# Another written-out order of the same steps on every engine of an RWKV-7 layer with a SwiGLU FFN

## What is computed

```
S_t = S_{t-1} * diag(exp(w_t)) + (S_{t-1} a_t) b_t^T + v_t k_t^T
y_t = S_t r_t          # then group norm, bonus term, gate, @ w_output.T
```

## Time and profile before

| | |
|---|---|
| device time, median of 3 runs | 1608.94 us (1607.33 to 1612.72) |
| span of the profiled execution | 1603.4 us |
| PE busy | 1520.5 us, 95% |
| DVE busy | 1243.6 us, 78% |
| ACT busy | 1069.5 us, 67% |
| POOL busy | 354.6 us, 22% |
| chain that ended last | PE 92%, DVE 3%, ACT 2% |

### The profile page before, as it was taken

One profiled execution on the slowest core, in us unless ns is written; L12 is line 12 of the kernel. 1 busy time (PEld: TensorE's weight loads), 2 busy tenths in 40 slices (PEclk: granted clock), 3 DMA queues, 4 the chain that ended last, 5 costly groups with the idle time before them and its releaser, 6 DMA issues.

```text
span 1603.4 us, 48245 instructions
## 1 busy us (share of the span) xinstructions
PE 1520.5 (95%) x20288; PEld 1064.9 (66%) x20288; DVE 1243.6 (78%) x2661; ACT 1069.5 (67%) x1889; POOL 354.6 (22%) x362
## 2 busy tenths in 40 slices
PE   3699999999999999999999999999999999999887
PEld 1366767576676757667676676757667675766765
DVE  2968787787878878887887878778787887888643
ACT  3758586685857758685775858668585775768512
POOL 3121402313040131302213140231304013130201
PEclk9799999999999999999999999999999999999999
DMA  4011110301212021111202111030121202111020
GB/s 149 14 25 29 33 34 16 62 18 32 43 25 47 16 55 25 33 34 24 56 16 39 42 34 34 16 62 19 33 42 25 48 16 55 25 33 34 12 56 28
DMA packets 251430, 57.85 MB, mean 36 GB/s; under 512 B 223696, under 2 KB 250704, under 8 KB 251088
## 3 DMA queue, kind: packets, MB, share of 16 engines
q1 hardware_dynamic: 241936, 41.95, 13.9%
q10 hardware_dynamic: 9280, 12.81, 2.2%
HBM read 36.38 MB, written 18.35 MB: 34 GB/s over the span
## 4 chain that ended last, share of the span: by engine, by line
PE 92%; DVE 3%; ACT 2%; issue 1%; POOL 0%; DMA 0%; SPq 0%; ACTq 0%; DVEq 0%; POOLq 0%
PE bank L534 23%; PE chunk L380 15%; PE bank L544 11%; PE bank L509 8%; PE bank L664 4%; PE chunk L642 3%; PE chunk L614 3%; PE chunk L589 3%; PE chunk L598 2%; PE bank L485 2%; PE bank L380 2%; PE bank L517 2%; PE bank L479 2%; PE chunk L628 2%; DVE VU L981 1%
## 5 line engine op out<-in xcount | busy, mean ns | idle before, releaser
L1325 POOL TENSOR_TENSOR SF<-ST,CT 128x256 f32<-128x256 f32 x128 | 99.7, 779 | 728.8 <-DVE ST L1211 728.8
L534 PE MATMUL bank<-xT,wg 128*128 128x256 f32 x768 | 197.2, 391 | 14.2 <-DVE VU L981 13.5
L534 PE MATMUL bank<-xT,wu 128*128 128x256 f32 x768 | 207.3, 395 | 0.0
L544 PE MATMUL bank<-wd,hT 128*128 128x256 f32 x768 | 176.8, 383 | 1.9 <-DVE hT L1171 1.9
L534 PEld LDWEIGHTS bank<-xT,wg 128*128 128x128 f32 x768 | 136.3, 189 | 57.6 <-DVE VU L981 24.1
L544 PEld LDWEIGHTS bank<-wd,hT 128*128 128x128 f32 x768 | 143.3, 190 | 29.3 <-issue 7.2
L534 PEld LDWEIGHTS bank<-xT,wu 128*128 128x128 f32 x768 | 135.1, 188 | 34.8 <-issue 14.5
L380 PE MATMUL chunk<-KS,W 128*128 128x512 f32 x320 | 149.6, 598 | 0.3 <-ACT gT L719 0.3
L509 PE MATMUL bank<-qpad,KS 128*64 128x32 f32 x4096 | 141.2, 226 | 4.0 <-DVE KE L1143 4.0
L887 ACT ACTIVATE Y<-chunk 32x256 f32<-32x256 f32 x256 | 96.3, 376 | 70.9 <-PE chunk L598 67.0
L509 PEld LDWEIGHTS bank<-qpad,KS 128*64 128x64 f32 x4096 | 130.7, 141 | 14.1 <-issue 9.0
(11 more groups left out here) (156 smaller groups left out, 3231.3 us busy)
## 6 DMA issues: line engine op xcount, KB each, us to landing
smalls<-in_x SPq DMA_DIRECT2D x32, 256.0 KB, 3.1
Y<-in_x SPq DMA_DIRECT2D x32, 256.0 KB, 3.0
out<-fsil ACTq DMA_DIRECT2D x32, 256.0 KB, 2.6
scrA<-AM SPq DMA_DIRECT2D x64, 64.0 KB, 1.9
hat<-scrB SPq DMA_DIRECT2D x32, 128.0 KB, 3.1
hat<-scrF SPq DMA_DIRECT2D x32, 128.0 KB, 3.1
KE<-scrA SPq DMA_DIRECT2D x64, 32.0 KB, 2.2
scrT<-KE SPq DMA_DIRECT2D x16, 128.0 KB, 1.7
```

Of the source, the lines that this page charges most:

```text
L534: q = pe.matmul(o[:, TT_ * n2:TT_ * n2 + TT_], w[:, h, 128 * (n + n2):128 * (n + n2) + 128], x_now[:, h], start=(h == 0), stop=(h == NH - 1))
L544: q = pe.matmul(o[:, 256 * m:256 * m + 256], hT[:, n, 128 * m:128 * m + 128], wd[:, n, :], start=(n == 0), stop=(n == NF - 1))
L1325: pool.tensor_tensor(SF[:, :, :, :], ST[:, :, :, :], fade[:, c].unsqueeze(3).to_broadcast([128, B, NH, N]), ALU.mult).then_inc(*faded.up)
```

## The change

```diff
-ORDER = {"pe": ("NNNFNKOOFNNORVNNNNKKOVKRBNKBNRNNVBBNBBNBNBNBBVNNBBEBVBBNBBVBNBBNBBXBXBBNXBBNBNBBXBBXBXBBNBBLBNBBXXBB"
-            "LXXXXLL"),
-         "act": ("NFKFFFFFRFVNKKNVOKKKBEBOKRKRDXXBXBVNBVNBBVVNBBBXBVVBBXBBBBNBBXXBLBBLXLBXBBNBBLXX"),
-         "dve": ("ONBOOBBBBBDBBBBBBBNBBDBBDDOOKKDXEFKKNDEDEXDKEEBXBXXXNBXBXXXBEXXBEXXBXNBXLBXXXBXXBLXBXNXXXBXXXBXLXLBX"
-             "XXBBXXLLLLLLLL"),
-         "pool": ("DBBBBBBLBBLBLLLLLLLL")}
-FIRST = {"pe": ("NFKFKKNNNNNVNNKVRKRVNRVVNNNNNNNNNNNNNNNNNVEXXXNXXXLXXXXXLXLLN"),
-         "act": ("NNKFFFNFNNFFKFKVKKKEVKKRRXXDRVVVVVVXXXNNXNLXXLLXXLX"),
-         "dve": ("DNDDDNFKKEDNKKDXEXDDENKEXXXLEXXXXXXLXXXEXEXXXXXXXXNXXXXXXXXXXXLLXXLLLLLLLNL"),
+ORDER = {"pe": ("NNFNNKOOFNNORKVNNONNKVKRBNKBNRNVNBBNBBNBNBNBBVNNBBEBNBBVBBVBNBBNBBXBXBBNBBNXBNBBXBBXBXBBNBBLBNBBXXBB"
+                "XLXXXLL"),
+         "act": ("NFKFFFFFFNROVONKKKKVKBEBKRRKXXXBVBDNBVNBBVVNBBBVXBBBBVBBXXBNBBBLBBXXLLXBNBBBBLXX"),
+         "dve": ("BOBNBBOBOBBBBBOBDFBBDBBBBNDOKKDEDKKNXDEDEXDKEEBXBXXXXBXNBEEXBXBXXXXXNBXBXLXBXBXXLXXXBNBXXXBXXXXXBLXX"
+                "BLXBBXLLLLLLLL"),
+         "pool": ("BDBBBLBBBLBBLLLLLLLL")}
+FIRST = {"pe": ("NFKNNFNKNKVKNVRRNNKRNVNNNVNVNVNENNXXXLNNXXXNNXXXNNXNXNNNLXLLN"),
+         "act": ("FKFFFFNFNKNFKVKKEKRVKKXRRXNNXDVVVNVVVXXLXLLXXXXLNXN"),
+         "dve": ("NDDDNFNDKEKDXNEKKDXEDDKEEXXXLXXXXLXEEXXXXXXXXXXXXXXXXXXXXXXXXLLXXLLLLLLNNLL"),
          "pool": ("DLLLLLLLLLL")}
-LAST = {"pe": ("NOOONONNNNNNNNNBBNNNBBBBBNBBBBBNBBBBBNBBBBBNBBBNBBNBBBBBNBBBBBNBBBNBBNNNNN"),
-        "act": ("NONNOBBNBBBBBBBBNBBBBBBBBBNBBBBBBBBNN"),
-        "dve": ("BOOOBBBBBBBBBBBBBBBBONONNBBBBBBBBBBBNBBBBBNBN"),
-        "pool": ("BBBBBBBBB")}
+LAST = {"pe": ("NNNNNONONNNONONNBBNNNBBBBBNBBBBBBBBNBBNBBBBBNBBBBBNBBBBBNBNBBNBBNBBBNBBNNN"),
+         "act": ("NNNBBOOBNBBBBBBBBBBNBBBBBBNBBBBBBNBBN"),
+         "dve": ("BONOOBBBBBBBBBBBBBBBBNOONBBBBBBBBBNBBBBBBNBNB"),
+         "pool": ("BBBBBBBBB")}
```

## The result

The changed kernel takes 1666.5 us (median of 4, 1664.6 to 1668.1) against 1610.8 us for the kernel before, run beside it (1607.3 to 1612.9): a ratio of 1.0353, 95% interval 1.0321 to 1.0385. The forecast was 1633 us, with a range up to 1644. The direction is right, and the loss is more than twice as large as predicted.

The account below looks back on a forecast made before the run. PE, busy 95% of the span, was taken as the bound; 26.6 (14 full sections) - 0.7 (section 0) - 1.7 (sections 16 and 17) = +24.2 us on 1608.94 gave 1633 us, own range 1623 to 1643, 8-in-10 range 1606 to 1644.

Parts of the forecast that it names:

- What bounds the kernel, and where the change bites: Whole kernel: PE, busy 95%, sets the time; full-section margins of z, yT0, out0 are 1.78, 0.96, 0.84 us.
- The turns and the new start: Start of full sections: unit, groupnorm and inv0 alternate with POOL's mixes; z 1.72 us later, 2.1 us per section.
- rule of hand-over: DVE and POOL, SBUF-only instructions: they run one after the other, and whoever waits gets the turn when the other's ends.
- Net per full section, +1.9: Sections 2 to 15: 2.1 us lost at the start, -0.2 from other moves; +26.6 us over 14 sections.
- a cause I have not counted: Full sections: a granted clock under 1.00 there would be a cause outside the forecast; no size given.
- The other moves: Rest of a full section: PE's exchanges cost 0, out1 earlier and short waits gone; -0.2 us, bounds -0.3 and +0.4.
- the thin margins: Full sections, behind the start: margins that get thin, such as u0 and s0 0.4 us later; upper bound +0.4 us.
- Section 0, -0.7: Section 0: lora first lets z start 1.3 us earlier, xT's transposes cost some; -0.7 us, bounds -1.4 and +0.5.
- Sections 16 and 17, -1.7: Last two sections: gate/up steps fill PE's early waits, recurrence starts some 2 us earlier; -1.7 us, bounds -3 and +0.7.
- The rivals: Whole kernel: three alternatives to the forecast, at 1603.7, 1609.3 and 1661 us, with chances 0.15, 0.12 and 0.08.
- Only groupnorm loses its turn: Rival, start of full sections: +0.4 - 0.2 us per section, 1609.3 us, no change; chance 0.12.
- The rival at 1661 us: Rival, recurrence: later DVE runs out of margin at u0, s0, u5 or s4, 2 us more per section; chance 0.08.

Follow-up runs that it names:

- the head alone: Kernel before with only the head of DVE's list in full sections changed (unit, groupnorm, inv0, up00, then yT0, yT1): 1657.8 us, ratio 1.0303.
- short mixes: Changed kernel with POOL's seventh and eighth mix in tiles 2 to 15 cut to 64 of 512 columns: 1620.2 us, ratio 1.0074.

## Why the prediction was wrong

**What bounds the kernel, and where the change bites**: right. PE has no slack, the change bites at the head of DVE's list, and `z`, yT0 and out0 are the late steps.

**The turns and the new start**: right, and close. Forecast was `z` 1.72 us later and out0 2.1; measured in section 11 are 1.90 and 2.02. The run with the head alone (97.0 us) and the one with short mixes bear out the mechanism. The rule of hand-over that I read from three rows (whoever waits gets the next turn) isn't always true: the blocked instructions of 4 us break it.

**Net per full section, +1.9**: this is the step that failed, in two ways. First, I priced PE's wait at its length ("each wait that PE gets in one section costs its length 14 times"). It costs the clock as well: 22.9 us over the span with the one blocked `unit` in it (about 1 us), more than half of the 38.5 us that were missing. The text names it as "a cause I have not counted". The signs were in rows of before: section 16, with waits of 3.3 and 2.6 us, has a mean clock of 0.92 with section 17, and I used that for section 16 alone.

The Trainium skill's page TensorE: Matmul & The Clock Gate (HAM oscillation) tells of a kernel whose clock falls once in each round of its loop behind a wait, and prices the slow time at half its length. By that, as an estimate, 3.4 us would cost 1.7 and 6.8 us 3.4; the rows say 1.1 and 2.7 to 2.9. Its kernel waited for DMA for longer than the 1.83 us seen here. What makes up a part of the difference shows in PE's rows: in section 5, with a fall, out0 starts 1.55 us later in the section than in section 11, but PE's wait of 0.33 us behind it (next paragraph) is gone.

Second, a section at full clock is 2.87 us longer and not 1.9. The other moves were costed at -0.2 with bounds -0.3 and +0.4; measured, what comes behind out0 is +0.85. Of it 0.33 us is `gh`, by a chain I left out: ACT's softplus for the decay writes the tile that DVE's `yT` reads, so ACT loads its table only behind the second `yT`, and PE's `gh` waits until the softplus has emptied its bank. The rows of ACT in section 5 after:

```profile
505.37 1.28 ACT L719 ACT_TABLE_LOAD   x1 [1.75 <-DVE hat L1238]
506.67 1.26 ACT L719 ACTIVATE gT<-chunk,nvec 128x512 f32<-128x512 f32 x2
```

Before, its margin on PE was 0.47 us; the second `yT` is 2.8 us late, as forecast (488.0 against 485.08), and out0's own 2.0 don't cover it. Another 0.35 is `rk`, 0.18 s3: the thin margins, which I had named, at +0.4 for all of them. PE's reordering gave back 0.1 at most.

**Section 0, -0.7**: not shown. Alone the strings give 1.0005 (0.9990 to 1.0020). Where the clock falls once ahead of section 1, section 0 takes 64.6 to 64.7 us with the new strings (four profiles) against 66.16 with the old (one, and 24 us at the lower clock in place of 17); over all profiles section 1 starts at 93.6 to 99.4 us with the new strings and at 95.4 to 101.3 with the old. **Sections 16 and 17, -1.7**: wrong sign. The early waits are filled, but as the prediction says PE then waits for up02 (3.2 us) and the loads behind flip (2.2 to 4.0), and the recurrence starts 0.9 to 2.3 us later, not 2 earlier; alone these strings cost 5.6 us (1.0035), though in the changed kernel's own profile the two sections are 0.6 us shorter. What they do to the recurrence's clock stays open.

**The rivals**: none came. "Only groupnorm loses its turn": the run with up00 before inv0 comes nearest to it, with `z` on time, and takes 97.89 us per section and not 95.3, since the `yT` stay behind the inv products. The rival at 1661 us was near in size, by another mechanism: its waits are 0.5 us per section, not 2. The range ended at 1644 because no case counted the clock, and it was too narrow even without it: up00 before inv0, with no fall in its profile's full sections, takes 1649.9 us.

## What to carry to other kernels

Where the bound engine gets a new wait in a loop, ask what it does to that engine's clock, and look in the trace for a place where it already waits that long; a wait of 1.8 us cost up to 4.7. Before pricing the removal of one late input, list all that are late together: with three in parallel, mending one left the section at 97.9 us and took away only the falls. To tell a wait from the clock behind it, fill the wait with harmless work: if the kernel gets faster with more matmuls, it was the clock.

## What the runs showed of the hardware

- The clock's fall at a wait of 1.83 us (with 0.25 and 0.89 us ahead of it) comes in most sections and not in all, with the same waits in each: 11 of 13 in the changed kernel, 10 of 14 with the head alone. Where PE idles as long in pieces of at most 1.0 us, it fell in 0 of 12 and 0 of 14 sections; where it waited 3.1 to 3.3 us in one piece, in 5 of 5. What decides it at 1.83 us stays open.
- A DVE instruction that waits for POOL usually starts when POOL's current one ends: groupnorm then takes 2.3 us behind a whole mix, 1.43 behind the end of one. Eight times in 224 starts of a section it was passed by all POOL instructions that were queued and took 4.6 to 5.6 us.
- Short steps of DVE beside a POOL instruction take nearly that one's length, however small they are: products of 15 columns 1.07 and 1.21 us beside mixes of 512 columns, 0.26 and 0.25 beside mixes of 64.
